# A selective scan and a mixture of experts: delta of two directions made inside the scan, down products in one run per weight set

## What is computed

```python
# 1. selective scan over D = 128 channels in K = 4 directions (rows, columns, each reversed), N = 16 states
xi, z = split(gn(x) @ in_proj);  xc = silu(conv3x3(xi) + b)
delta_k = softplus(dt_w[k] @ dts_k + dt_b[k])
h = exp(delta*A)*h + (delta*u)*B_n ;  y += h*C_n      # for every state n, along the 256 tokens
x = x + ((sum over k of y_k + Ds*u_k) * silu(z)) @ out_proj
# 2. attention over a band of 7 tokens, on layer-normed tokens
# 3. E = 8 experts of 682 hidden units, all computed densely; gates keep the two largest softmax values
h = silu(f @ w1[e].T) * (f @ w3[e].T);  out += gate[e] * (h @ w2[e].T)
```

## Time and profile before

| what | value |
|---|---|
| median of three runs | 250.86 us (250.72 to 251.13) |
| the profiled execution | 253.52 us, of which the span of instructions is 251.8 |
| mean granted TensorE clock | 0.964 |
| busy: TensorE, VectorE, ScalarE, GpSimd | 222.2, 179.3, 137.8, 139.1 us |
| first `times_b` to the last scan's end | 30.80 to 142.88 us |
| attention block, router product | to 168.1 us |
| experts | 168.1 to 249.6 us |

### The profile page before, as it was taken

How to read it: one execution, slowest core, us unless ns; L and a number is a source line. 1 busy time by engine, 2 the same in 40 slices (tenths; PEclk the granted TensorE clock), 3 DMA queues, 4 the chain that set the end, 5 groups by cost and what they waited for, 6 DMA issues and landing times. The chain is left out here.

```text
span 251.8 us, 2856 instructions
## 1 busy us (share of the span) xinstructions
PE 222.2 (88%) x738; PEld 96.3 (38%) x738; DVE 179.3 (71%) x280; ACT 137.8 (55%) x204; POOL 139.1 (55%) x135
## 2 busy tenths in 40 slices
PE   7989849999789987998776999993999999999992
PEld 2323213423234232423222255662444555554530
DVE  4504997999999999999999654368654463544642
ACT  4136995967768876896657323453232433444430
POOL 5620999777998789977999900008007608400000
PEclk9999986999999999999999998999599999999999
DMA  5699300000000000000000900000900200100000
GB/s 152 140 209 207 55 0 1 3 1 0 0 0 0 0 0 0 3 0 1 1 0 9 215 0 3 0 0 0 211 14 0 56 0 16 42 0 0 0 0 21
DMA packets 8004, 8.56 MB, mean 34 GB/s; under 512 B 6646, under 2 KB 7223, under 8 KB 7480
## 3 DMA queue, kind: packets, MB, share of 16 engines
q1 hardware_dynamic: 7992, 8.42, 15.4%
HBM read 8.29 MB, written 0.13 MB: 33 GB/s over the span
## 5 line engine op out<-in xcount | busy, mean ns | idle before, releaser
L404 POOL TENSOR_TENSOR rings<-rings 128x512 f32<-128x512 f32 x64 | 80.1, 1271 | 12.4 <-DVE rings L652 12.1
L879 PE MATMUL ps<-rings,ident 128*128 128x512 f32 x128 | 70.7, 634 | 12.7 <-POOL rings L404 12.2
L652 DVE TENSOR_TENSOR_SCAN rings<-rings,ps 128x512 f32<-128x512 f32 x64 | 76.0, 1208 | 0.2 <-ACT rings L502 0.2
L807 DVE TENSOR_TENSOR gl<-ps,si 128x512 f32<-128x512 f32 (+1 forms) x44 | 30.4, 691 | 35.5 <-ACT si L565 35.4
L565 ACT ACTIVATE si<-ps 128x512 f32<-128x512 f32 (+1 forms) x44 | 26.2, 597 | 46.7 <-PE ps L1014 42.4
L502 ACT ACTIVATE rings<-delta,a_neg 128x510 f32<-128x510 f32 x64 | 44.1, 712 | 3.3 <-DVE rings L652 3.0
L510 ACT ACTIVATE rings<-ps 128x1024 f32<-128x1024 f32 x32 | 32.6, 1018 | 22.9 <-POOL rings L404 22.9
L645 DVE TENSOR_TENSOR ps<-ps,du 128x512 f32<-128x512 f32 x64 | 42.4, 686 | 2.0 <-PE ps L891 1.8
L879 PEld LDWEIGHTS ps<-rings,ident 128*128 128x128 f32 x128 | 22.0, 193 | 40.4 <-POOL rings L404 36.3
L421 POOL TENSOR_TENSOR wup<-wraw,wup 64x2728 fp32r<-64x2728 f32 x3 | 18.1, 6026 | 25.0 <-issue 24.8
L1014 PE MATMUL ps<-fh,wup 128*128 128x512 f32 (+1 forms) x88 | 31.3, 437 | 0.7 <-DVE gl L807 0.7
(11 more groups left out here) (172 smaller groups left out, 187.9 us busy)
## 6 DMA issues: line engine op xcount, KB each, us to landing
wraw<-w_up_dram SPq DMA_DIRECT2D x8, 682.0 KB, 7.2
wdn<-w_down_dram SPq DMA_DIRECT2D x4, 160.0 KB
w_conv<-conv_w_dram SPq DMA_DIRECT2D x1, 576.0 KB, 4.4
wdn<-w_down_dram SPq DMA_DIRECT2D x4, 128.0 KB
xg<-x_grp_dram SPq DMA_DIRECT2D x1, 128.0 KB, 2.7
xc<-x_chan_dram SPq DMA_DIRECT2D x1, 128.0 KB, 3.0
xt<-x_tok_dram SPq DMA_DIRECT2D x1, 128.0 KB, 2.0
out_dram<-res SPq DMA_DIRECT2D x1, 128.0 KB, 1.7
```

Of the source, the lines that this page charges most:

```text
L404: nc.gpsimd.tensor_tensor(hc[:, q], hs[:, q], cs[:, q], ALU.mult).then_inc(weighted, 1)
L652: nc.vector.tensor_tensor_scan(hs[:, q, :], da[:, q].rearrange("p b l -> p (b l)"), driven(q), 0.0, ALU.mult, ALU.add).then_inc(scanned, 1)
L807: nc.vector.tensor_tensor(gl[0:rows, S % 4, :], ps[0:rows, BANK_H + 2 * (S % 3) + 1, :], si[0:rows, S % 2, :], ALU.mult).then_inc(glu_read ...
L879: nc.tensor.matmul(ps[:, BANK_Y, :], ident[:], hc[:, q % BODY, :], start=False, stop=last_state).then_inc(y_ready if last_state else summe ...
```

## The change

The delta work of directions 2 and 3 (and max(x,0) of 1 to 3, the flips, the second half's dt rows) moves from the front into written-out scan bodies; `keep_part` of direction 0 and |x| of 0 and 1 stay ahead of the scan on VectorE. The hidden products get 16 buffers in the scan's rings, and the six `downs` of a set stand in one run behind step 1 of the next set (four of the last set behind its step 9). VectorE splits set 1's low half behind steps 0 to 3 of set 0, and the gate chain starts at step 4.

```diff
+GATED = 4 * BODY
...
-ROUND_AT = [(1, 0), (1, 3), (2, 0), (2, 3)]
+ROUND_AT = [40, 45, 49, 53]
...
+        gated = rings[:].rearrange("p r (q t) -> p (r q) t", q=BODY)
...
-            return (len(PIECE_AT) if pair % 2 == 0 else 1) + pair // 2
+            return 4 + pair // 2
...
-        BANKS_DT = (7, 3, 4, 6)
-        BANKS_DTR = (5, 1)
-        BANKS_IN = (0, 1, 3, 7)
+        BANKS_DT = (7, 3, 2, 2)
+        BANKS_DTR = (5, 2)
+        BANKS_IN = (0, 1, 7, 3)
...
-                    pool.wait_ge(above_kept, len(above))
+                    pool.wait_ge(above_kept, k)
...
-                    pool.wait_ge(u_ready, K)
+                    pool.wait_ge(u_ready, (3, 2, 4)[k - 1])
...
+                    if k == 0:
+                        if n == 3:
+                            prepare(1, 0)
+                        elif n == 5:
+                            prepare(1, 1)
+                        elif n == 12:
+                            prepare(1, 2)
+                        elif n == 13:
+                            rounding_of(2, 0)
+                        elif n == 15:
+                            rounding_of(2, 1)
+                    elif k == 1:
+                        if n == N + 1:
+                            rounding_of(3, 0)
+                        elif n == N + 3:
+                            rounding_of(3, 1)
+                        elif n == N + 5:
+                            prepare(2, 0)
+                        elif n == N + 8:
+                            prepare(2, 1)
+                        elif n == N + 10:
+                            prepare(2, 2)
+                    elif k == 2:
+                        if n == 2 * N + 1:
+                            prepare(3, 0)
+                        elif n == 2 * N + 3:
+                            prepare(3, 1)
+                        elif n == 2 * N + 6:
+                            prepare(3, 2)
+                    elif n in PIECE_AT:
                         low_piece(PIECE_AT.index(n), n)
...
+            pool.wait_ge(du_ready, 1)
+            rounding_of(1, 0)
+            rounding_of(1, 1)
+            states_loop(nc.gpsimd, body, written_out=range(K))
 
 
...
-            for pair in range(1, PAIRS):
-                if pair >= 2:
-                    pool.wait_ge(raw_in[pair % 2], 32 * (pair // 2 + 1))
-                    pool.wait_ge(up_ready, STEPS * (pair - 1))
-                    nc.gpsimd.tensor_copy(wup[:, pair % 2], wraw[:, pair % 2]).then_inc(w_rounded, 1)
+            for pair in range(2, PAIRS):
+                pool.wait_ge(raw_in[pair % 2], 32 * (pair // 2 + 1))
+                pool.wait_ge(up_ready, STEPS * (pair - 1))
...
+            keep_dtr(0)
...
+            exp_part(0)
+            exp_part(1)
+            nc.scalar.preload_act_table_set("natural_log")
+            log_part(0)
+            log_part(1)
             nc.scalar.preload_act_table_set("exp_and_others")
...
+                    if k == 0 and n == 1:
+                        keep_above(1)
...
+                    if k == 0:
+                        if n == 2:
+                            keep_dtr(1)
+                        elif n == 5:
+                            magnitude(2)
+                        elif n == 6:
+                            keep_above(2)
+                        elif n == 8:
+                            magnitude(3)
+                        elif n == 9:
+                            keep_above(3)
+                        elif n == 10:
+                            exp_part(2)
+                        elif n == 11:
+                            keep_flipped(1)
+                        elif n == 12:
+                            exp_part(3)
+                        elif n >= 13:
+                            keep_part(1, n - 13)
+                    elif k == 1:
+                        if n == N + 6:
+                            nc.scalar.preload_act_table_set("natural_log")
+                            log_part(2)
+                            log_part(3)
+                            nc.scalar.preload_act_table_set("exp_and_others")
+                        elif n in (N + 3, N + 10, N + 13):
+                            keep_part(2, (N + 3, N + 10, N + 13).index(n))
+                    elif k == 2:
+                        if n == 2 * N + 2:
+                            keep_flipped(3)
+                        elif n in (2 * N + 6, 2 * N + 9, 2 * N + 12):
+                            keep_part(3, (2 * N + 6, 2 * N + 9, 2 * N + 12).index(n))
+                    if n in ROUND_AT:
+                        half = ROUND_AT.index(n)
                         act.wait_ge(raw_in[half // 2], 32)
                         nc.scalar.activation(wup[:, half // 2, half % 2], wraw[:, half // 2, half % 2],
                                              ACT.Copy).then_inc(w_rounded, 1)
...
+            keep_first_part(0)
+            magnitude(0)
+            magnitude(1)
+            dve.wait_ge(aexp_ready, 1)
+            nc.vector.tensor_scalar(a_neg[:], a_exp[:], -1.0, None, ALU.mult).then_inc(aneg_ready, 1)
+            keep_first_part(1)
...
+            keep_first_part(2)
...
+            def low_piece(piece):
+
+                dve.wait_ge(w_rounded, rounds_through(1))
+                low = (slice(C, 2 * C), 1, piece // 2, piece % 2)
+                nc.vector.tensor_tensor(wup[low], wraw[low], wup[low].bitcast(FP32), ALU.subtract).then_inc(slot_ready[1], 1)
...
-                    if S >= 4:
-                        dve.wait_ge(down_done, groups_through(S - 4))
-                    nc.vector.tensor_tensor(gl[0:rows, S % 4, :], ps[0:rows, BANK_H + 2 * (S % 3) + 1, :],
+                    if S >= GATED:
...
-                    if pair == 0:
-                        gate_step(s)
+                    if pair == 0 and s < 4:
+                        low_piece(s)
+                    elif pair == 0:
+                        gate_step(s - 4)
...
+                    if k == 0 and n == 2:
+                        pe.wait_ge(delta_ready, 1)
+                        keep_warm(5, BANKS_DT[0])
+                    elif k == 0 and n == 3:
+                        pe.wait_ge(above_kept, 1)
...
+                    if k == 0:
+                        if n == 3:
+                            pe.wait_ge(dtr_kept, 2)
+                            dt_product(2)
+                        elif n == 7:
+                            pe.wait_ge(above_kept, 2)
+                            dt_product(3)
+                        elif n == 10:
+                            pe.wait_ge(above_kept, 3)
+                            flip_channels(0)
+                        elif n == 12:
+                            pe.wait_ge(u_ready, 3)
+                            project(1)
+                        elif n > 12 and n < 15:
+                            take_off(1, n - 12)
+                    elif k == 1:
+                        if n == N + 2:
...
-            pe.wait_ge(u_ready, 2)
-            pe.wait_ge(z_done, 1)
-            dt_rows(1)
...
-                    if s >= 3 and s % 2:
-                        downs(pair, (s - 3) // 2)
-                    if pair and s < 2:
-                        downs(pair - 1, GROUPS - 2 + s)
+                    if pair and s == 1:
+                        for j in range(GROUPS):
+                            downs(pair - 1, j)
+                    if pair == PAIRS - 1 and s == STEPS - 2:
+                        for j in range(GROUPS - 2):
+                            downs(pair, j)
```

More of the change, by code:

```diff
@@ L460, in keep_part @@
             def keep_part(k, part):
-                if isinstance(part, int) and part == 0:
+                if part == 0:
                     act.wait_ge(proj_ready, k + 1)
@@ L520, in _ @@
             act.wait_ge(da_zero, 1)
-            states_loop(nc.scalar, body)
+            states_loop(nc.scalar, body, written_out=range(K))
             nc.scalar.preload_act_table_set("sqrt_and_others")
@@ L659, in body, with keep_first_part, magnitude @@
                 scan(BODY - 1)
-            for k in range(K):
+            def keep_first_part(part):
+                if part == 0:
+                    dve.wait_ge(proj_ready, 1)
+                else:
+                    dve.wait_ge(rest_ready, part)
+                nc.vector.tensor_copy(bc[:, 0, :], ps[0:6 * N, BANK_B, :]).then_inc(part_kept, 1)
+            def magnitude(k):
                 dve.wait_ge(dt_ready, k + 1)
@@ L666, in _ @@
                                         ALU.bitwise_and).then_inc(abs_ready, 1)
-            def keep_above(k):
-                nc.vector.tensor_scalar(above[k], ps[:, BANKS_DT[k], :], 0.0, None, ALU.max).then_inc(above_kept, 1)
-            keep_above(3)
-            prepare_first()
-            keep_above(1)
+            keep_first_part(0)
[4 more added lines that the diff above has]
+            keep_first_part(1)
+            rounding = rd[:, 0, :]
+            dve.wait_ge(ex_ready, 1)
```

(14 more changed lines are left out.)

111 lines of the change are left out of this document (44 added, 67 removed).

## The result

| | before, beside it | changed |
|---|---|---|
| median | 251.0 us (250.72 to 251.57, four runs) | 248.6 us (247.52 to 249.41, four runs) |
| ratio | | 0.9899, 95% interval 0.9856 to 0.9941 |
| the profiled execution | 253.52, span 251.8, clock 0.964 | 249.41, span 247.7, clock 0.985 |
| first `times_b` / last sum's start | 30.80 / 144.69 | 26.49 / 141.15 |
| first up product of the experts | 168.15 | 164.60 |

All ratios leave out an execution that took over 1.5% longer than the fastest of its kernel.

What follows compares the result with a forecast made beforehand. VectorE's two operations a state were taken to bound the scan, TensorE the experts. Scan's end (-4.2 + 0.6 + 1.6 = -2.0) and experts (-4.8) took 253.5 to 246.7 profiled, 244.1 for the median; range 240.5 to 248.0.

Steps and rivals of the forecast that it cites:

- Front (-4.2): Before the scan: VectorE's shortened chain brings the first state from 30.80 to 26.6, bounds -3.6 and -4.5.
- Scan (+0.6, +1.6): Scan: TensorE's added products cost 0.6 (bounds -2.4, +3), GpSimd's late products 1.6 (bounds 0, 3.2).
- I keep the 2.4 and add 0.6: Direction 0 still loses 2.4 as before, plus 0.6 for one product falling into the slow stretch at double length.
- the three guests: dt of 2 and 3 and the flip, on TensorE in states 3 to 10 of direction 0, each 1.0 at full clock.
- Set 0 (-4.4): Experts' start: the GpSimd jam and slow stretch go, so the first turn stands at 194.2 instead of 198.6.
- The last rival: Set 0: GpSimd's copy of set 2's weights holds VectorE, making the kernel slower; +9.8, 253.9; chance 0.08.
- The forecast's own 0.9 of waiting in step 14: Set 0's end: products 11 and 12 come at 191.9 and 192.5, so TensorE's step 14 waits 0.9.
- The rival's own price, +9.8: Set 0, VectorE held by the copy: the run starts 7.9 late and the fallen clock costs 2.8; chance 0.08.
- A step with a piece: Set 0, steps 0 to 3: VectorE's product at pitch 0.61 plus a 682-column piece at 0.78, so 1.4 a step.
- The run (-0.7 a set, +1.0 in the last): Later sets: six down groups together at 0.87 each save 0.7 a set, twice; four groups behind the last turn cost 1.0.
- the carried difference: Profiled execution 253.52 against median 250.86: the 2.66 between them was carried over to the changed kernel.

Runs made afterwards that it cites:

- experiment 2: Changed kernel, with GpSimd's copy and subtraction of set 2's weights held back until set 0's products are done: 244.67 us, ratio 0.9725.
- experiment 5: Changed kernel, with GpSimd's copy of set 2's weights at its old place and only the subtraction held back behind the gate chain: 248.29 us, ratio 0.9850.
- experiment 6: Changed kernel without GpSimd's wait for du of direction 0 ahead of its rounding of direction 1: 248.91 us, ratio 0.9899.
- experiment 9: Changed kernel, set 1's low half on GpSimd, gate chain in first run, set 2's GpSimd work behind it, turn after step 5, addition after 6 and 8: 236.68 us.
- experiment 4: Changed kernel, with GpSimd's work on set 2's weights held back and one down group after every second step instead of the run: 242.67 us, ratio 0.9664.
- 10: Changed kernel, with single down groups, set 2's GpSimd work held back, set 1's low half as one early GpSimd subtraction: 242.22 us, ratio 0.9629.
- kernel 8: Changed kernel, run kept, set 1's low half on GpSimd, gate chain in the first run, set 2's GpSimd work behind it: 243.88 us, ratio 0.9667.

## Why the prediction was wrong

**Front (-4.2): right.** First state at 26.49 against 26.6, each intermediate time within 0.15.

**Scan (+0.6, +1.6): GpSimd's term right, TensorE's mis-sized.** 1.67 was waited for GpSimd's late products, 1.6 forecast. Of the 3.0 that direction 0 was to lose it lost 1.1. The term that failed is "I keep the 2.4 and add 0.6": I took the half clock of one execution for a property of the kernel, and let it last as long as in the earlier trace rows. The same scan lost nothing, about 1.1 or about 2.2 over its first 16 states, depending on the execution. That this profile lost only 1.1 was luck of the execution. At the full clock the three guests fit. The experts' first product comes 3.55 earlier, 2.0 was forecast: 1.55 in my favour.

**Set 0 (-4.4): failed, measured -0.94** (30.40 to 29.46), and +0.2 against the second profile of before (29.25). This is the step that made the prediction wrong: the forecast had the first turn 26.05 behind the first up product (194.2 - 168.15), and with the collision away it came at 26.26 (experiment 2). That the two nearly agree is in part luck. The forecast's own 0.9 of waiting in step 14 fell away, and the pieces took 0.9 more. In detail:

- The last rival was the mechanism, and I had given it 0.08. My forecast let the copy pass beside VectorE and held only the last gate step, by the subtraction. In fact the copy held the sum of two one-hots (2.34) and the subtraction held the next operation with two SBUF inputs (5.41); experiment 5 shows that the copy does it by itself, experiment 2 that the whole costs 3.2 up to the first turn. The reason that I gave against it, an operation of 0.68 inside GpSimd's scalar operation, was true but of another kind of GpSimd operation. The trace of before couldn't settle it: beside the copy of the earlier trace rows VectorE has only products with one operand in PSUM, which are not held (0.69), and its operations with two SBUF inputs all stand elsewhere. A question that no row answers was worth more than 0.08. What the Trainium skill states (SBUF — State Buffer, Who interferes with whom), that GpSimd's reads go through VectorE's second port pair under an exclusive lock, covers the copy; experiment 5 agrees, 2.33 us held under a copy of 2.49. One of the products beside the copy of the earlier trace rows, from VectorE's timeline of before:

```profile
192.04 0.69 DVE L807 TENSOR_TENSOR gl<-ps,si 128x512 f32<-128x512 f32 x1 [0.24 <-ACT si L565]
```

- The rival's own price, +9.8, was as wrong as its chance. It let the first operation be caught earlier in the chain and two products stand behind the second, and added a fallen clock at 2.8 (its parts, 3.7 - 2.0 and 1.9 - 1.0, add to 2.6). The copy started at 179.96, behind step 10, when the comparison had just started; one product got through between copy and subtraction (182.53), which released TensorE's last up step; five of the six groups could run meanwhile, so that TensorE was busy in 5.16 of the 6 us behind 184. The clock stayed at 1.00 in this execution and fell to 0.50 in experiment 6; there the first turn came 29.96 behind the first up product, 0.5 later.
- A step with a piece was taken at 1.4 and took 1.62, four times, 0.9 in all. I had added two pitches, and a pitch is less than a duration only where neighbours overlap. The piece works on partitions 64 to 127, the product on 0 to 127, and they follow one another at 0.72 and 0.90, no shorter than themselves. The Trainium skill (VectorE: DVE Perf Modes, Two Vector instructions with no wait between them) says that an instruction whose SBUF input or output starts in another quadrant of 32 partitions than that of the instruction before it is held until every earlier one has finished; the trace agrees, with these 0.2 a step.

**The run (-0.7 a set, +1.0 in the last): right in size for the run, half given back.** The sets came out at -0.38 each (-0.7 forecast) and the last at +1.13 (+1.0). The run itself was worth more than I took: without the waits a set takes 16.43 (experiment 9), 1.45 less than before. The waits behind it took 1.05 of that, where I had put 0.95. What I missed is in set 0, inside the -4.4: there a run is a loss, 1.3 up to the first turn (experiment 4), since TensorE's gaps between slow steps were free places for the groups.

**Profile and median: failed.** Of the 4.5 by which the median missed, 1.85 are the carried difference. The sum against the profiled execution was 246.7 and the profile gave 249.41, 2.7 more: 4.25 too little in the experts (set 0 3.5, later sets 0.65, last set 0.1) less 1.55 from the scan. The profiled execution of before had a clock of 0.964, and the runs' spread went with the clock; a term that rests on a half-clock stretch may not be used in the sum and be taken off again as the difference of profile and median.

So the sign came from the front and the scan (in the profiles with some luck of the clock), and the experts' part of the change did nothing as built: its stop was moved and not removed. With VectorE's operations moved clear of GpSimd's long ones, or to where holding them costs nothing, and with the turn later, the kernel comes to 0.9424 of before (experiment 9).

## What to carry to other kernels

Before an operation is moved, list every long GpSimd operation and every VectorE operation with two SBUF inputs in its new neighbourhood, copies included; moving one out of a jam puts its followers into the next. A run of equal matmuls saves at TensorE, but only where TensorE is the bound, and its consumers (a transpose, an addition) must be moved later with it: the same run cost 2.0 us against single groups with its turn and addition at the old steps, and the kernel with the gate chain in the run and both moved later beat single groups by 5.5 (experiments 9 and 10). That pair differs in three things at once, and single groups with the gate chain elsewhere weren't tried. When executions of one kernel differ in granted clock, read the gain from stretches at equal clock, and don't carry the profile's distance to the median over.

## What the runs showed of the hardware

- GpSimd's copy of 128 x 2728 (one SBUF input) held a VectorE operation of 32 columns for 2.33 and 2.34 us, to its own end, as its two-input subtraction did for 3.4, 5.4 and 2.8.
- GpSimd's scalar operation of 512 columns held VectorE little or not at all: 0.68 and 0.98 for VectorE operations with two SBUF inputs beside it that take 0.69. Why it differs from the copy wasn't tried.
- VectorE's product with one operand in PSUM wasn't held by the copy (0.69 at 192.04, inside the copy of the earlier trace rows).
- The hold goes both ways: GpSimd's operation of 1.27 took 2.19 beside a VectorE sum that took its usual 0.68, and then held VectorE's next product to 1.65 (experiment 6).
- The kernel before ran between 250.3 and 255.5 us with clocks of 0.950 to 0.977. Half clock in the attention block (0.52 at 152 to 155 in the changed kernel) is there in one execution and not in the next of the same instructions: from the sum at 135.13 (kernel 8) and 134.42 (kernel 9), the same sum near the scan's end, to the first up product 29.58 and 27.94 passed.
